# A new order of steps in a transformer encoder kernel, and one mask seed each moved to VectorE and to TensorE

## The chip, the cores and the metric
The kernel runs on one core of a Trainium2 chip. Five engines work side by side, each through its own list of instructions, and wait for each other by semaphores: TensorE (PE; matrix products into PSUM), VectorE (DVE), ScalarE (ACT; activations, with function tables that have to be loaded), GpSimd (POOL) and SyncE (SP), which here issues transfers. The metric is the time of one execution on the device in microseconds (us), lower is better.

## The reference
The input is 16 sequences of 256 rows of 128 numbers. A first layer norm gives `xn`; the result is `x + encoder(xn) + experts(xn)`. The encoder has four layers; in each:

```python
xn = layer_norm(x, ln1_w[i], ln1_b[i])
x = x + mha(xn, mask, in_proj_w[i], in_proj_b[i], out_proj_w[i], out_proj_b[i])
xn = layer_norm(x, ln2_w[i], ln2_b[i])
h = jax.nn.gelu(xn @ ffn1_w[i].T + ffn1_b[i], approximate=False)
x = x + (h @ ffn2_w[i].T + ffn2_b[i])
```

`mha` is attention with 16 heads of width 8, a causal mask and a linear position bias; a final layer norm closes the encoder. The experts are one attention of 8 heads over the same rows, with projections cut to segments, and no feed-forward.

## The kernel before
One sequence in one layer is a **unit**: the encoder has 64 of them (4 layers x 16 sequences), the experts 16. The kernel is a software pipeline written by hand: slot `s` of a plan holds, one after another, steps of the units s-2 to s+3, and every engine walks through the same list (`slot_steps`) and issues of each step its own part. So the list sets the order on each engine, and an engine that waits for a step holds up all that stands behind it in its list. Two slots make a round; the rounds stand in loops.

The way of a unit: `ln`, `rstd`, `xn` (norm, on VectorE and POOL), `xt` and `xt+` (transpose on TensorE; scale and bias on ScalarE), `qk` and `y` (queries and keys; their bias on ScalarE), `hi` and `lo` (split into two parts for precision), `hi>` (both parts to DRAM), `smax>`/`smaxp` and `stack>` (transfers that stack them per head, by SyncE and POOL; the first two for the maxima, the last for the scores), 12 steps `max` (score products with the mask as a second product `identb` x `maskb`, line 1022, and a reduction on VectorE, line 768), `negt`, `negt+`, `row>` (the row of negated maxima, as a row of the queries), 12 steps `exp` (a 128x512 score product, line 1052, and the exponential on ScalarE, line 918), four steps `pv` (probabilities by values, line 1075, in column strips of 32), `pv+` (copy, line 818), `ot`, `ot+` (division by the sums), `at`, `at+`, `op`, `op+` (projection and residual), `rstd2`, `xn2`, `xt2`, `xt2+`, `f1` and `gelu` in two halves of two blocks, `f2` in two halves, `f2+`. In the last layer `end` and `end+` work the final norm and `store` writes it.

**Seeds.** Of the 12 score tiles of a unit, 8 cross the diagonal (numbers 0, 2, 3, 5, 6, 8, 9, 11). For these ScalarE first writes the mask `masktf` into the PSUM bank (line 943) and the score product adds to it. There are two such banks (`exp_ps`), used in turn, so the seed of tile k+2 follows the exponential of tile k, and waits for its end. `SEEDER` names the engine for each tile.

**Banks.** Seven more PSUM banks: 0 and 1 (`dense`), 2 to 4 (`mxp`), used by the maxima in turn (2 + k % 3), and one for `pv`. `Plan.banks` gives each other step its bank; `take` makes TensorE wait until the last reader of a bank is done. Before, `xt`, `qk`, `negt`, `f2` use bank 1, `v`, `at`, `op`, `xt2` bank 0, `ot` bank 4, `f1` banks 0 and 1.

Of the kernel before, what the change touches and what calls it, by code (L numbers as in the profile page):

```python
# [22 lines left out]
BF16 = mybir.dt.bfloat16  # L23
# [4 lines left out]
P = 128  # L28
# [23 lines left out]
class Plan:  # L52
# [21 lines left out]
    def slot_steps(self, s, last_layer):  # L74
# [3 lines left out]
        def at(names, unit):  # L78
            return [(name, unit) for name in names.split()]
# [4 lines left out]
        if self.causal:  # L84
            end, end2, store = (at(k, s - 2) if last_layer else [] for k in ("end", "end+", "store"))
            return (
                part("exp", s, 0, 1) + at("ot", s - 1) + at("ln rstd", s + 2) + at("ot+", s - 1) + at("v v+", s + 1)
                + at("w:v xn", s + 2) + part("f2", s - 2, 0, 1) + at("w:w2", s - 1) + at("f2+", s - 2)
                + end + at("at at+", s - 1)
                + part("exp", s, 2) + at("w=w1", s - 1) + part("max", s + 1, 0, 1) + at("xt", s + 2)  # L90
                + part("exp", s, 3) + part("max", s + 1, 2, 3) + at("xt+", s + 2) + at("op xb", s - 1)
                + at("stack>", s + 1)
                + part("exp", s, 4) + at("w=v", s + 2) + part("max", s + 1, 4) + at("op+ rstd2 w=w2 xb2", s - 1)
                + at("w:o", s) + at("qk", s + 2)
                + part("exp", s, 5) + part("max", s + 1, 5, 6) + at("y", s + 2) + at("w:qk", s + 3)
                + at("hi lo hi>", s + 2)
                + part("exp", s, 6) + part("max", s + 1, 7, 8) + end2 + at("xn2", s - 1)
                + part("exp", s, 7) + part("max", s + 1, 9, 10)
                + part("exp", s, 8) + part("max", s + 1, 11)
                + part("exp", s, 9) + at("w=o", s) + at("xt2 xt2+", s - 1) + part("pv", s, 0, 1)  # L100
                + part("exp", s, 10) + at("w=qk", s + 3) + at("negt negt+ row>", s + 1) + at("smaxp smax>", s + 2)
                + part("exp", s, 11) + part("f1", s - 1, 0, 1) + part("gelu", s - 1, 0, 1) + at("w:w1", s)
                + part("pv", s, 2, 3) + at("pv+", s) + store)
# [25 lines left out]
    "xt": 1, "qk": 1, "v": 0, "at": 0, "op": 0, "xt2": 0, "negt": 1, "f2": 1, "ot": 4, "f1": (0, 1)})  # L129
# [1099 lines left out]
```

## Time and profile before

| | |
|---|---|
| median of 3 runs | 1633.32 us (1630.77 to 1640.77) |
| profiled execution | 1632.11 us |
| its span | 1630.3 us |
| granted TensorE clock, mean over the span | 0.968 of full speed |
| TensorE / ScalarE / VectorE busy | 1420.4 / 1225.0 / 1124.3 us |

A timeline row gives start, duration, engine, line, operation, tiles written and read, shapes and count, and in brackets how long the engine was idle before it and what ended this. Rows of one kind in a row are merged. Matmuls are pipelined: the duration of one is from its start to its modelled end, and the distance of two ends is what it adds. The chain of work that ended last is followed back from the last instruction to what released each step; its pieces are such distances.

### The profile page before, as it was taken

To read this page: it belongs to the slowest core of one execution; us is meant where nothing else is said; L and a number is where in the kernel's file an instruction comes from. 1 tells how busy PE (TensorE), PEld (TensorE's weight loads), DVE (VectorE), ACT (ScalarE), POOL (GpSimd) and SP (SyncE) were. 2 spreads that over 40 slices of the span, in tenths; PEclk is the share of its full clock that TensorE was granted. 3 is DMA by queue.
4 is the path that set the end of the run, shared out by engine and by line. 5 is a ranking of instruction groups with operands and counts; after the bars stand their busy time and mean duration, and the time that the engine had idled before them with its cause. 6 is when DMAs were issued, how large, how long until landed. Compare 5 with 4: busy or idle time off the path is not lost.

```text
span 1630.3 us, 39578 instructions
## 1 busy us (share of the span) xinstructions
PE 1420.4 (87%) x10656; PEld 949.4 (58%) x10720; DVE 1124.3 (69%) x2850; ACT 1225.0 (75%) x2165; POOL 613.5 (38%) x1052
## 2 busy tenths in 40 slices
PE   0677787679999999999999999999999999999994
PEld 0445554346666666666666666666666666666653
DVE  6566666457777777777777767777677777777762
ACT  3233333248889889999898888888989888888883
POOL 5232323223334333333333333333333345555533
PEclk9899889789999999999999999999999999999997
DMA  4333333144444444544444445444444444444430
GB/s 131 101 103 93 104 90 114 43 128 125 119 118 117 125 131 120 141 129 118 119 130 121 123 117 135 125 127 117 120 128 128 128 129 123 122 123 123 125 85 11
DMA packets 106535, 187.80 MB, mean 115 GB/s; under 512 B 20104, under 2 KB 72456, under 8 KB 106448
## 3 DMA queue, kind: packets, MB, share of 16 engines
q1 hardware_dynamic: 91632, 150.45, 33.3%
q0 software_dynamic: 14848, 36.72, 8.4%
q8 instruction: 21, 0.34, 0.1%
q14 instruction: 34, 0.28, 0.1%
HBM read 120.87 MB, written 65.01 MB: 114 GB/s over the span
## 4 chain that ended last, share of the span: by engine, by line
PE 52%; DVE 18%; issue 14%; DMA 8%; POOL 1%; ACT 1%; SPq 1%; DVEq 1%; POOLq 0%; ACTq 0%
PE pvp L1075 12%; PE exp_ps L1052 7%; DVE negm L768 7%; PE mxp L1018 6%; PE dense L1116 5%; PE dense L1104 5%; DMA blocks<-split_L 5%; PE dense L964 5%; PE mxp L1022 2%; DVE xn L736 2%; PE dense L1093 2%; DVE ost L818 2%; PE mxp L964 2%; PE dense L1003 2%; PE dense L993 2%
## 5 line engine op out<-in xcount | busy, mean ns | idle before, releaser
L918 ACT ACTIVATE probs<-exp_ps 128x512 f32<-128x512 f32 x896 | 525.7, 593 | 283.6 <-PE exp_ps L1052 279.7
L768 DVE TENSOR_REDUCE negm<-mxp 128x2 f32<-128x512 f32 x896 | 568.4, 682 | 74.1 <-remote 38.3
L1052 PE MATMUL exp_ps<-qbd_l,kst_l 128*128 128x512 f32 x768 | 367.8, 495 | 9.6 <-issue 5.0
L1018 PE MATMUL mxp<-blocks,qst 104*128 104x512 f32 x768 | 326.4, 453 | 29.7 <-DVE negm L768 16.5
L943 ACT ACTIVATE exp_ps<-masktf 128x512 f32<-128x512 f32 x513 | 308.8, 602 | 22.6 <-DVE rest L840 6.4
L556 POOL TENSOR_SCALAR veps<-mv 128x2 f32<-128x2 f32 x144 | 31.7, 220 | 540.5 <-DVE mv L727 537.2
L1022 PE MATMUL mxp<-maskb,identb 128*128 128x256 bf16 (+1 forms) x704 | 222.1, 315 | 0.0
L818 DVE COPY ost<-pvp 128x512 f32<-128x512 f32 x80 | 55.3, 691 | 205.6 <-PE pvp L1075 205.6
L1018 PEld LDWEIGHTS mxp<-blocks,qst 104*128 104x128 f32 x768 | 148.5, 193 | 83.0 <-DVE negm L768 43.4
L1075 PE MATMUL pvp<-probs,vst_l 128*32 128x256 f32 (+1 forms) x4096 | 194.2, 330 | 0.6 <-ACT probs L918 0.6
L1052 PEld LDWEIGHTS exp_ps<-qbd_l,kst_l 128*128 128x128 f32 x768 | 144.4, 195 | 41.1 <-issue 32.7
L1022 PEld LDWEIGHTS mxp<-maskb,identb 128*128 128x128 bf16 x768 | 75.1, 98 | 156.9 <-issue 135.1
L1075 PEld LDWEIGHTS pvp<-probs,vst_l 128*32 128x32 f32 x4096 | 115.1, 110 | 77.6 <-ACT probs L918 26.3
L592 POOL TENSOR_TENSOR lo<-y,hi 128x512 fp32r<-128x512 f32 x80 | 102.6, 1283 | 134.8 <-DVE hi L743 134.8
L736 DVE TENSOR_SCALAR xn<-state,mv,rstd 128x128 f32 (+1 forms) x288 | 133.6, 503 | 20.6 <-POOL rstd L558 19.1
L964 PE MATMUL dense<-ident,xn 128*128 128x128 f32 x288 | 62.4, 301 | 77.9 <-DVE xn L736 73.1
L1116 PE MATMUL dense<-wc_l,hid 128*128 128x128 f32 x1024 | 124.9, 274 | 1.0 <-ACT hid L939 1.0
L1104 PE MATMUL dense<-xnt,wc_l 128*128 128x256 f32 x512 | 122.6, 383 | 0.7 <-ACT xnt L932 0.7
L623 POOL DMA_DIRECT2D blocks<-split_L x128 | 68.8, 544 | 144.0 <-DVE negt L807 113.2
L1116 PEld LDWEIGHTS dense<-wc_l,hid 128*128 128x128 f32 x1024 | 119.5, 192 | 1.7 <-ACT hid L939 1.6
L558 POOL TENSOR_TENSOR rstd<-veps,half 128x2 f32<-128x2 f32 x144 | 102.7, 713 | 12.0
L1104 PEld LDWEIGHTS dense<-xnt,wc_l 128*128 128x128 f32 x512 | 98.3, 192 | 14.2 <-ACT xnt L932 1.1
(94 smaller groups left out, 2014.0 us busy)
## 6 DMA issues: line engine op xcount, KB each, us to landing
split_L<-hi SPq DMA_DIRECT2D x256, 128.0 KB, 2.1
qst<-split_L SPq DMA_DIRECT2D x64, 384.0 KB
kst_l<-split_L SPq DMA_DIRECT2D x64, 384.0 KB
qbd_l<-split_L SPq DMA_DIRECT2D x256, 96.0 KB
split_L<-lo POOLq DMA_DIRECT2D x128, 128.0 KB, 2.1
blocks<-split_L POOLq DMA_DIRECT2D x128, 96.0 KB, 4.3
blocks<-split_L SPq DMA_DIRECT2D x128, 96.0 KB
split_F<-hi SPq DMA_DIRECT2D x64, 128.0 KB, 2.1
```

The source lines that it names most:

```text
L558: pool.tensor_tensor(rstd[:, k, s, :], veps[:, k, s, :], half[:, 0:NT], ALU.pow).then_inc(done, 1)
L736: last = dve.tensor_scalar(xn[:, k, s, t, :], source[:, t, :], mv[:, k, s, t, 0:1], rstd[:, k, s, t:t + 1], ALU.subtract, ALU.mult)
L768: dve.tensor_reduce(heads[:, g, first:first + count], bank[MAX_BANK + k % 3].rearrange("p (h t) -> p h t", h=count), AX.X, ALU.max, negate ...
L918: act.activation(probs[:, g, ch, :], exp_ps[:, k % 2, :], ACT.Exp, scale=plan.scale).then_inc(q.b_exp, 1)
L943: act.activation(exp_ps[:, bank, :], masktf.rearrange("p h t -> p (h t)"), ACT.Copy)\
L964: last = pe.transpose(out_bank[0:src.shape[1], k * width:(k + 1) * width], src, ident[:, :])
L1018: pe.matmul(o, qst[0:BIAS_END, g, qt * P:(qt + 1) * P], kbd[0:BIAS_END, first:first + count, g, 0:keys], start=True, stop=True, skip_group ...
L1022: last = pe.matmul(diagonal, identb[:, :], maskb[:, 0:count, :], start=False, stop=True, skip_group_check=True)
L1052: last = pe.matmul(o, kst[plan.name][:, s, g, kt * P:(kt + 1) * P], rhs, start=seeder not in ("ACT", "DVE"), stop=True, skip_group_check=True)
L1075: last = pe.matmul(pvp[32 * col:32 * col + 32, region * T + q0:(region + 1) * T], v, src, start=lead, stop=fin_, skip_group_check=True, ti ...
L1104: last = pe.matmul(o[:, (f % 2) * T:(f % 2 + 1) * T], wc["L"][:, C_W1 + f * P:C_W1 + (f + 1) * P], xnt[:, 1, s, :], start=True, stop=True)
L1116: last = pe.matmul(o[:, k * D:(k + 1) * D], hid[:, s, f, k * P:(k + 1) * P], wc["L"][:, C_W2 + f * D:C_W2 + (f + 1) * D], start=(f == 0), ...
```

## The change
The list of a slot is written anew for the encoder (the experts' stays), the banks of its steps are other ones, seed 0 goes to VectorE (the list has a `seed` step for it, for unit s+1, in front of `pv 3`), tile 2 is no longer seeded: after its score product TensorE adds `identb` x `masktb`, a bfloat16 copy of the mask that POOL makes once. POOL's share of the final norm (`end_rstd`, `end_sum`) becomes steps of their own at the end of a slot.

```diff
         if self.causal:
...
             return (
-                part("exp", s, 0, 1) + at("ot", s - 1) + at("ln rstd", s + 2) + at("ot+", s - 1) + at("v v+", s + 1)
-                + at("w:v xn", s + 2) + part("f2", s - 2, 0, 1) + at("w:w2", s - 1) + at("f2+", s - 2)
-                + end + at("at at+", s - 1)
...
+                at("w:v", s + 2) + at("w:w1", s - 1) + at("w:qk", s + 3) + at("w:o", s) + part("f1", s - 2, 1)
+                + at("hi>", s + 2) + at("w=o", s) + at("w=w1", s - 1) + at("v", s + 1) + at("xn", s + 2)
+                + at("at+ ot", s - 1) + at("xt", s + 2) + at("ot+", s - 1) + at("v+", s + 1) + part("f2", s - 2, 0)
+                + at("at", s - 1) + at("xt+", s + 2) + at("ln", s + 3)
+                + part("exp", s, 0, 1) + at("stack>", s + 1) + at("w:w2", s - 1) + at("w=v", s + 2) + at("w=qk", s + 3)
+                + at("op+ op", s - 1) + at("qk", s + 2) + part("max", s + 1, 0) + at("y", s + 2) + part("max", s + 1, 1)
...
+                + part("exp", s, 11) + at("lo", s + 2) + part("gelu", s - 1, 0) + at("negt+ negt", s + 1)
+                + part("gelu", s - 1, 1) + part("pv", s, 2) + part("seed", s + 1, 0) + part("pv", s, 3) + at("pv+", s)
+                + at("row>", s + 1) + store + at("xb", s) + at("rstd", s + 3) + end_rstd + end_sum)
...
-    "xt": 1, "qk": 1, "v": 0, "at": 0, "op": 0, "xt2": 0, "negt": 1, "f2": 1, "ot": 4, "f1": (0, 1)})
+    "xt": 0, "qk": 4, "v": 4, "at": 2, "op": 2, "xt2": 0, "negt": 3, "f2": 1, "ot": 3, "f1": (0, 1)})
...
-SEEDER = {0: "ACT", 2: "ACT", 3: "ACT", 5: "ACT", 6: "ACT", 8: "ACT", 9: "ACT", 11: "ACT"}
+SEEDER = {0: "DVE", 2: "PE", 3: "ACT", 5: "ACT", 6: "ACT", 8: "ACT", 9: "ACT", 11: "ACT"}
...
+                        if seeder == "PE":
+                            last = pe.matmul(o, identb[:, :], masktb.rearrange("p h t -> p (h t)"), start=False, stop=True,
+                                             skip_group_check=True)
```

On ScalarE, from the GELU of one unit into the next, in the last rounds (written out, without a loop); before:

```order
L939 ACTIVATE hid<-dense,wc_l 128x256 x4
L918 ACT_TABLE_LOAD
L918 ACTIVATE probs<-exp_ps 128x512
L943 ACTIVATE exp_ps<-masktf 128x512
L918 ACTIVATE probs<-exp_ps 128x512
L943 ACTIVATE exp_ps<-masktf 128x512
L925 ACTIVATE attnt<-dense 128x256
L918 ACTIVATE probs<-exp_ps 128x512 x2
```

and now (line numbers are those of the changed kernel, 4 higher):

```order
L943 ACTIVATE hid<-dense,wc_l 128x256 x4
L929 ACTIVATE attnt<-mxp 128x256
L908 ACTIVATE xnt<-dense,wa_l 128x256
L922 ACT_TABLE_LOAD
L922 ACTIVATE probs<-exp_ps 128x512 x2
L947 ACTIVATE exp_ps<-masktf 128x512
L915 ACTIVATE y<-mxp,wa_l 128x256 x2
L922 ACTIVATE probs<-exp_ps 128x512 x2
```

The attention copy and the normalised input now stand ahead of the table load and the first exponential; exponential 0 has no seed behind it.

On TensorE, the same place; `dense<-xnt,wc_l` is `f1`, `dense<-wc_l,hid` is `f2`; before:

```order
L964 MATMUL dense<-ident,negm 16x128 x2
L1052 MATMUL exp_ps<-qbd_l,kst_l 128x512
L1104 MATMUL dense<-xnt,wc_l 128x256 x4
L1075 MATMUL pvp<-probs,vst_l 32x256 x4
L1075 MATMUL pvp<-probs,vst_l 32x128 x4
L1075 MATMUL pvp<-probs,vst_l 32x256 x4
L1075 MATMUL pvp<-probs,vst_l 32x128 x4
L1052 MATMUL exp_ps<-qbd_l,kst_l 128x512 x2
L964 MATMUL mxp<-ident,ost 128x128 x4
L1003 MATMUL dense<-wa_l,xnt 128x128 x2
L1116 MATMUL dense<-wc_l,hid 128x128 x8
L964 MATMUL dense<-ident,attn 128x128 x2
```

and now:

```order
L968 MATMUL mxp<-ident,negm 16x128 x2
L1082 MATMUL pvp<-probs,vst_l 32x256 x4
L1082 MATMUL pvp<-probs,vst_l 32x128 x4
L1082 MATMUL pvp<-probs,vst_l 32x256 x4
L1082 MATMUL pvp<-probs,vst_l 32x128 x4
L1111 MATMUL dense<-xnt,wc_l 128x256 x2
L1007 MATMUL mxp<-wa_l,xnt 128x128 x2
L968 MATMUL mxp<-ident,ost 128x128 x4
L968 MATMUL dense<-ident,xn 128x128 x2
L1123 MATMUL dense<-wc_l,hid 128x128 x4
L968 MATMUL mxp<-ident,attn 128x128 x2
L1056 MATMUL exp_ps<-qbd_l,kst_l 128x512 x2
```

One half of `f1` moved behind the last `pv`, the score products 0 and 1 moved behind `ot`, `xt`, the first half of `f2` and `at`.

On TensorE a few steps on; before, `qk` (`dense<-xnt,wa_l`) stands between maxima 4 and score 5:

```order
L1022 MATMUL mxp<-maskb,identb 128x2x128
L993 MATMUL dense<-xnt,wa_l 128x256 x2
L1052 MATMUL exp_ps<-qbd_l,kst_l 128x512
L1018 MATMUL mxp<-blocks,qst 128x512
L1022 MATMUL mxp<-maskb,identb 128x2x128
L1018 MATMUL mxp<-blocks,qst 128x512
L1022 MATMUL mxp<-maskb,identb 128x512
L1052 MATMUL exp_ps<-qbd_l,kst_l 128x512
```

and now `op` and `qk` stand ahead of maxima 0, and score 2 has a mask product:

```order
L1100 MATMUL mxp<-wc_l,attnt 128x128 x2
L997 MATMUL mxp<-xnt,wa_l 128x256 x2
L1022 MATMUL mxp<-blocks,qst 128x512
L1026 MATMUL mxp<-maskb,identb 128x512
L1022 MATMUL mxp<-blocks,qst 128x512
L1026 MATMUL mxp<-maskb,identb 128x2x128
L1056 MATMUL exp_ps<-qbd_l,kst_l 128x512
L1059 MATMUL exp_ps<-masktb,identb 128x512
L1056 MATMUL exp_ps<-qbd_l,kst_l 128x512
L1022 MATMUL mxp<-blocks,qst 128x512
L1026 MATMUL mxp<-maskb,identb 128x2x128
L1022 MATMUL mxp<-blocks,qst 128x512
```

`qk` writes bank 4, which maxima 2 (the third `mxp<-blocks,qst` row) use next.

## Rows read from the trace of the kernel before

**Rows 1.** The page: busy times; and the chain that ended last, by engine.
```profile
PE 1420.4 (87%) x10656; PEld 949.4 (58%) x10720; DVE 1124.3 (69%) x2850; ACT 1225.0 (75%) x2165; POOL 613.5 (38%) x1052
...
PE 52%; DVE 18%; issue 14%; DMA 8%; POOL 1%; ACT 1%; SPq 1%; DVEq 1%; POOLq 0%; ACTq 0%
```

**Rows 2.** Timeline, VectorE, line 818: start us, us, engine, line, operation, count, [idle before, releaser].
```profile
359.17 0.69 DVE L818 COPY ost<-pvp 128x512 f32<-128x512 f32 x1 [2.09 <-PE pvp L1075]
...
1339.54 0.69 DVE L818 COPY ost<-pvp 128x512 f32<-128x512 f32 x1 [2.92 <-PE pvp L1075]
...
1602.68 0.69 DVE L818 COPY ost<-pvp 128x512 f32<-128x512 f32 x1 [7.66 <-PE pvp L1075]
```

**Rows 3.** Timeline, ScalarE, from one unit's end into the next.
```profile
708.25 0.60 ACT L918 ACTIVATE probs<-exp_ps 128x512 f32<-128x512 f32 x1 [0.85 <-PE exp_ps L1052]
...
710.02 1.28 ACT L939 ACT_TABLE_LOAD   x1
711.32 1.56 ACT L939 ACTIVATE hid<-dense,wc_l 128x256 f32<-128x256 f32 x4
...
714.19 0.60 ACT L918 ACTIVATE probs<-exp_ps 128x512 f32<-128x512 f32 x1
714.82 0.60 ACT L943 ACTIVATE exp_ps<-masktf 128x512 f32<-128x512 f32 x1
715.36 0.58 ACT L918 ACTIVATE probs<-exp_ps 128x512 f32<-128x512 f32 x1
...
716.51 0.37 ACT L925 ACTIVATE attnt<-dense 128x256 f32<-128x256 f32 x1
...
716.77 1.26 ACT L918 ACTIVATE probs<-exp_ps 128x512 f32<-128x512 f32 x2
...
718.60 0.55 ACT L904 ACTIVATE xnt<-dense,wa_l 128x256 f32<-128x256 f32 x1
...
721.16 0.83 ACT L911 ACTIVATE y<-dense,wa_l 128x256 f32<-128x256 f32 x2
```

**Rows 4.** Chain in order of time, 700 to 740 us: start us, us, what.
```profile
707.79 0.43 PE exp_ps L1052
...
708.67 1.73 PE dense L1104 x8
710.40 1.48 PE pvp L1075 x32
...
713.82 1.79 PE dense L1116 x16
715.61 0.22 PE dense L964 x2
715.83 0.23 PE exp_ps L1052
...
717.63 0.12 PE mxp L1022
717.76 0.23 PE mxp L1018
717.99 0.23 PE mxp L1022
718.22 0.44 PE dense L1093 x4
```

**Rows 5.** Timeline, TensorE: a product that waited for ScalarE.
```profile
719.29 1.10 PE L993 MATMUL dense<-xnt,wa_l 128*128 128x256 f32 x4
```

**Rows 6.** The page, costliest groups: shapes, count | busy, mean ns | idle before.
```profile
L768 DVE TENSOR_REDUCE negm<-mxp 128x2 f32<-128x512 f32 x896 | 568.4, 682 | 74.1 <-remote 38.3
```

**Rows 7.** Chain in order of time, 789 to 812 us: a transfer.
```profile
788.61 5.20 DMA blocks<-split_L
```

**Rows 8.** Timeline, VectorE, in the tail.
```profile
1610.49 0.42 DVE L830 TENSOR_TENSOR state<-dense,xb 128x256 f32<-128x256 f32 x1 [2.93 <-POOL xb L635]
```

More of the change, by code:

```diff
@@ L84, in slot_steps @@
         if self.causal:
-            end, end2, store = (at(k, s - 2) if last_layer else [] for k in ("end", "end+", "store"))
+            end, end_rstd, end2, end_sum, store = (
+                at(k, s - 2) if last_layer else [] for k in ("end", "end_rstd", "end+", "end_sum", "store"))
             return (
-                part("exp", s, 0, 1) + at("ot", s - 1) + at("ln rstd", s + 2) + at("ot+", s - 1) + at("v v+", s + 1)
-                + at("w:v xn", s + 2) + part("f2", s - 2, 0, 1) + at("w:w2", s - 1) + at("f2+", s - 2)
-                + end + at("at at+", s - 1)
[L90 to L103, printed above, removed]
@@ new lines, in slot_steps @@
+                + at("op+ op", s - 1) + at("qk", s + 2) + part("max", s + 1, 0) + at("y", s + 2) + part("max", s + 1, 1)
+                + part("exp", s, 2, 3) + part("max", s + 1, 2) + at("hi", s + 2) + part("max", s + 1, 3)
+                + part("exp", s, 4) + part("max", s + 1, 4) + part("pv", s, 0) + part("max", s + 1, 5, 6)
+                + part("exp", s, 5, 6) + part("f2", s - 2, 1) + at("xn2", s - 1) + at("f2+", s - 2)
+                + end + at("smaxp", s + 1)
+                + part("exp", s, 7) + part("max", s + 1, 7, 8) + at("xb2", s - 1) + part("max", s + 1, 9)
@@ new lines, in slot_steps @@
+                + part("exp", s, 8) + at("xt2+", s - 1) + part("pv", s, 1) + at("smax>", s + 2) + at("w=w2 xt2", s - 1)
+                + part("max", s + 1, 10)
+                + part("exp", s, 9) + at("rstd2", s - 1) + part("max", s + 1, 11) + end2
+                + part("exp", s, 10) + part("f1", s - 1, 0)
+                + part("exp", s, 11) + at("lo", s + 2) + part("gelu", s - 1, 0) + at("negt+ negt", s + 1)
+                + part("gelu", s - 1, 1) + part("pv", s, 2) + part("seed", s + 1, 0) + part("pv", s, 3) + at("pv+", s)
@@ L316, in build @@
         masktf = sb("masktf", [P, 4, P])
+        masktb = sb("masktb", [P, 4, P], BF16)
         split = {p.name: nc.dram_tensor(f"split_{p.name}", [2, 2, p.hg, COPIES, p.dh, GROUPS * T], F32,
@@ L566, in steps @@
                         inverse_deviation(q, "C", u, s)
-                    elif step == "end":
+                    elif step == "end_rstd":
                         b = u - (LAYERS - 1) * BATCH
@@ L577, in steps @@
                         pool.tensor_tensor(rest[:, b, :, :], rest[:, b, :, :], bias, ALU.add).then_inc(s_end_rest, 1)
-                    elif step == "end+":
+                    elif step == "end_sum":
                         b = u - (LAYERS - 1) * BATCH
@@ L1137, in encoder @@
                 next_round(n)
-            pe.wait_ge(s_init, 12)
+            pe.wait_ge(s_init, 13)
             pe.wait_ge(s_initv, 1)
```

1 line of the change is left out of this document (added).

## The prediction

> **What bounds the kernel now.** The busy times first [rows 1]: TensorE 87% of the span, ScalarE 75%, VectorE 69%. Nothing is full, so the chain of work that ended last decides: TensorE holds 52% of it, VectorE 18%, "issue" 14%, DMA 8%, ScalarE 1%. The encoder repeats one pattern, once for each of its 64 units. The copy of a unit's attention output (line 818) marks one period [rows 2]: from 359.17 to 1339.54 us there are 50 periods, mean 19.61 us; then 13 to 1602.68, mean 20.24 us, in which the final norm is worked too. Before them lie 359 us (experts and filling), behind them 27.6 us. The span is 1630.3 us and the profiled execution 1632.1 us; the median of the runs shown is 1633.32, so 1.2 us above it.
>
> Inside a period TensorE's own work, taken from end to end of its products [rows 4]: 12 score products at 0.23, 12 maxima products at 0.23 with 4 masks at 0.23 and 8 at 0.12, values and output projection 0.44 each, queries and keys 0.87 (half of the 1.73 for the first feed-forward, which has twice the products), feed-forward 1.73 and 1.79, four probability-value steps at 0.74, six pairs of transposes at 0.22. That is about 17.0 us. The other 2.3 to 2.6 us are waits and refills. One wait shows the price of a refill [rows 3, 5]: the activation begun at 718.60 ends at 719.15, the product that waited ends at 719.29+1.10 = 720.39, 1.24 us later, for 0.87 of streaming: 0.37 extra. And the score product behind a probability-value step ends 0.43 after it, where 0.23 is normal [rows 4]: 0.20 for leaving that step.
>
> **The change, part by part.** (1) Two of eight seeds leave ScalarE. A seed followed by another activation takes 714.82 to 715.36 = 0.54 us, and it delays the exponential ahead of it to 0.63 [rows 3]; so 2 x 0.6 = 1.2 us less per unit on an engine that holds 1% of the chain [rows 1]. Alone this gains nothing. (2) One seed goes to VectorE, after the copy of negated maxima: not in the trace; at least nothing, since the engine idles 31% of the span; at most about 0.69 us, the 128x512 copy with one side in PSUM [rows 2], its nearest row, which I take. It runs while TensorE does the last probability-value step, whose copy stands behind it and can't begin before T+1.1 (T is where a unit's last exponential ends). Hidden. (3) One seed becomes a mask product: 0.23 us as the same 128x512 mask [rows 4].
>
> (4) The order. I walk one period with the durations of [rows 3, 4]; times are from T.
> ScalarE: table load and four GELU activations end at 2.88 in before (710.02 less 0.02 is T there). Now TensorE did score product 11 (ends T-0.62: 0.03 [rows 3, 4] and the exponential of 0.58), transposes 0.22 and pv 2, 0.74, so at 0.34 it starts pv 3: 1.08, leaving it 1.28, second half of feed-forward 1 (0.87): 2.15. The second GELU pair starts at 2.2 and not 2.10: end 2.95. Values, two pairs of transposes and one more take TensorE to 3.25.
> The first half of feed-forward 2 needs the GELU: 2.95+0.37+0.90 = 4.2. Behind it in TensorE's queue stands the transpose of attention: 4.42. And ScalarE has, ahead of its first exponential, what waits for this: the attention copy (starts 4.46; the next activation 0.26 later), the normalised input (0.55, ends 5.27), the table load (1.28) [rows 3]. Exponential 0 starts at 6.58. In before it started at 4.19 (714.19 against 710.00). These 2.4 us of delay are the change's largest cost.
> Then exponential 1 at 7.12, seed 3 at 7.75 (ends 8.35), the pair of query and key activations 8.29 to 9.12 [rows 3]. TensorE meanwhile ends queries and keys at 5.27+1.24 = 6.51, maxima 0 and 1 at 7.33, score 2 with its new mask at 8.0, and waits for seed 3: score 3 ends 8.35+0.37+0.23 = 8.95. Maxima 2 now uses the bank of queries and keys (bank 4), so it waits for both activations: 9.12+0.37+0.23 = 9.72.
> From there TensorE streams: its mask 0.12, eight scores 1.84, six maxima with short mask 2.22, three with long 1.38, pv 0 and pv 1 1.48, leaving each 0.40, half of feed-forward 2 0.90, transposes 0.22, half of feed-forward 1 0.87: 9.43 in all, end 19.15. ScalarE is ready there (six seeds keep it below this). Plus 0.62 to the end of exponential 11: **T+19.77**.
>
> So the gains (normalised input ready early, pv 2 ahead of the last exponential, the projection's waits gone from VectorE's queue) about equal the losses: a mask 0.23, two places more on the stream where a pv step is left, 0.40, and the two waits before maxima 2. VectorE's twelve reductions at 0.68 [rows 6] are followed by the copy of high parts, norm and residual; the latest reduction that TensorE needs (maxima 8 for 11) ends over 1 us ahead in my walk. With 0.4 us less slack it would show.
>
> (5) Transfers. In before a DMA row of 5.20 us [rows 7] ends where maxima 0 start, one reason why the mean is 19.61. Now SyncE issues the stack for maxima ahead of the row of maxima, hence about 1.6 us before T, and maxima 0 start at 6.5, not 5.9: this wait should go. SyncE's queue stacks queries and keys behind the high parts (about T+13 to 15.5): 8 us ahead of their use. If that cover were gone, the row of maxima would be late next, then score 0.
> (6) Tail: an addition waited 2.93 us for POOL's xb, which stood behind the final norm [rows 8]; xb is now made a slot earlier: -3 us. Experts unchanged.
>
> Sum against the profiled execution: 50 x (19.77 - 19.61) = +8; 13 periods with the final norm: POOL and VectorE carry the same work, +1; tail -3. 1632.1 + 6 = **1638 us**.
>
> A rule speaks of the price of leaving a step. What rows show: pv steps take 1.48 for two with no visible price on entering, 0.20 on leaving [rows 4]. The Trainium skill, TensorEngine Tiling (Array Packing), Key Properties, says that a change of tiling mode drains TensorE; that would count on entering as well. By this reading two more entries on the stream cost some 0.2 each; the trace agrees for leaving alone.
>
> **The rivals.** (a) Leaving costs nothing here: the 0.20 is seen only where a score product follows; now maxima, transposes and feed-forward follow. Then the stream is 0.40 shorter and the GELU 0.07 earlier: T+19.30, (19.30-19.61) x 50 = -15, 13 x -0.3 = -4, tail -3: **1610**. For it: no row of another follower; against: it is an idle of the array, not a wait of the score. (b) ScalarE was the bound and the two seeds pay in full: 64 x 1.2 = -77: **1555**. Against: 1% of the chain. (c) Entering costs 0.20 too at pv 0 and pv 1: 63 x 0.4 = +25: **1663**, slower. It decides from 0.15 per entry on. Against: 1.48 for two steps. (d) The high parts, the stack of queries and keys and the low parts now move together; if the low parts land later than about T+20.5, SyncE's stack for maxima and the row behind it hold up score 0, by 1 us per us: +1 gives **1701**. For it: the 5.20 us row; against: 3 us of slack. (e) In the last 13 periods POOL's blocks stand behind the final sum, which now comes after all maxima: up to 1 us each, **1651**. (f) The order doesn't matter, as both are bound by the same work: **1633**.
>
> **How the numbers follow.** Forecast 0.40, (a) 0.20, (b) 0.06, (c) 0.11, (d) 0.09, (e) 0.06, (f) 0.08. The forecast's own range is 1622 to 1652 (0.25 us per period either way, the refills of a walk). The range of 8 in 10 reaches past (a) and (c), each with the forecast's own error of a few us: 1598 to 1670; it leaves out (b) and (d). About 1% is what a measurement of this kernel can tell from no change. Faster by over 1% (under 1617): (a), (b), some of the forecast's edge, 0.27. Slower (over 1649.7): (c), (d), half of (e), edge: 0.27. Within: 0.46.
>
> **What would show it.** Period of line 818's successor near 19.8, with little spread; exponential 0 starting 6.4 to 6.8 us after the last exponential's end, ScalarE idle 1.5 us behind the GELU; score 3 and maxima 2 each with an idle, ended by ScalarE; no maxima product waiting for DMA; the product behind each pv step 0.20 late; the seed on VectorE 0.6 to 0.7. Wrong if the first exponential starts before 6, or if TensorE waits after maxima 2: then VectorE or a transfer is the bound.

## The result

The changed kernel takes 1648.74 us, median of 4 runs (1646.89 to 1654.01); the kernel before took 1632.05 us beside it (1629.61 to 1640.77, 4 runs). The ratio is 1.0098, with a 95% interval of 1.0053 to 1.0143: about 1% slower, 10.7 us above the 1638 that the prediction names. Its profiled execution took 1647.52 us, with a span of 1645.0.

The page of the changed kernel, busy times and the chain by engine, answers to [rows 1]:
```profile
PE 1446.2 (88%) x10719; PEld 956.2 (58%) x10784; DVE 1143.3 (69%) x2914; ACT 1146.8 (70%) x2036; POOL 610.3 (37%) x1053
...
PE 63%; ACT 11%; issue 8%; DMA 8%; DVE 4%; SPq 1%; POOL 1%; ACTq 1%; another core or an unknown queue 0%; DVEq 0%; POOLq 0%
```
TensorE works 26 us more, and ScalarE 78 us less, but the two have changed their place in the chain: VectorE's share went from 18% to 4%, and ScalarE, which has less to do than before, now holds 11% of it instead of 1%.

The copies that mark the periods (now line 822), first, 51st and last, in VectorE's timeline of the changed kernel, answer to [rows 2]:
```profile
363.77 0.69 DVE L822 COPY ost<-pvp 128x512 f32<-128x512 f32 x1 [0.45 <-PE pvp L1082]
...
1364.66 0.69 DVE L822 COPY ost<-pvp 128x512 f32<-128x512 f32 x1 [0.36 <-PE pvp L1082]
...
1621.39 0.69 DVE L822 COPY ost<-pvp 128x512 f32<-128x512 f32 x1 [2.31 <-PE pvp L1082]
```
From these starts the span divides as follows (before by [rows 2]):

| stretch | before, us | after, us | difference |
|---|---|---|---|
| up to the first copy | 359.17 | 363.77 | +4.6 |
| 50 periods | 980.37 (19.61 each) | 1000.89 (20.02 each) | +20.5 |
| last 13 periods | 263.14 (20.24 each) | 256.73 (19.75 each) | -6.4 |
| behind the last copy | 27.6 | 23.6 | -4.0 |
| span | 1630.3 | 1645.0 | +14.7 |

The undisturbed periods of the changed kernel alternate between 19.85 and 19.98 us; seven of the first 50 are longer (20.19 to 22.49). Of the last 13, the two at the end are short in both kernels (19.56 and 18.88 before, 19.45 and 17.88 after), since the pipeline runs empty there.

ScalarE's timeline of the changed kernel, from the end of a unit's last exponential (T = 741.36) into the next unit, answers to [rows 3]:
```profile
742.68 1.65 ACT L943 ACTIVATE hid<-dense,wc_l 128x256 f32<-128x256 f32 x4
745.95 0.39 ACT L929 ACTIVATE attnt<-mxp 128x256 f32<-128x256 f32 x1 [1.63 <-PE mxp L968]
746.25 0.56 ACT L908 ACTIVATE xnt<-dense,wa_l 128x256 f32<-128x256 f32 x1
746.83 1.28 ACT L922 ACT_TABLE_LOAD   x1
748.12 1.09 ACT L922 ACTIVATE probs<-exp_ps 128x512 f32<-128x512 f32 x2
749.24 0.60 ACT L947 ACTIVATE exp_ps<-masktf 128x512 f32<-128x512 f32 x1
749.78 0.82 ACT L915 ACTIVATE y<-mxp,wa_l 128x256 f32<-128x256 f32 x2
```
The engine idles 1.63 us behind the GELU, until TensorE has multiplied with its result and transposed. Then it works without a gap, and what it does last there, `y` at 749.78, is what TensorE waits for. The chain in order of time, the same period, answers to [rows 4]:
```profile
742.38 1.06 PE dense L1111 x4
...
744.54 1.06 PE dense L1123 x8
...
750.65 0.50 PE mxp L1022
...
752.34 0.79 PE pvp L1082 x16
753.12 0.43 PE mxp L1022
...
757.13 0.79 PE pvp L1082 x16
757.92 0.37 PE dense L968 x2
...
759.48 0.86 PE dense L1111 x4
760.35 0.36 PE exp_ps L1056
```
From 750.65 on no other engine stands in the chain up to the last score (760.71): this is the stream. What TensorE waited for between 600 and 1200 us, in total, times, longest:
```profile
PE exp_ps L1056 <- DMA qbd_l<-negt: 18.6, 17, 2.4
PE exp_ps L1056 <- ACT exp_ps L947: 6.1, 18, 0.4
PE mxp L1022 <- ACT y L915: 5.4, 21, 0.3
```
The first of the three is new: the first score of a unit waits for the row of negated maxima. In most periods it costs nothing, since maximum 2 waits for `y` behind it anyway: in the period shown score 0 waited 0.59 us for the row, and the period is an undisturbed one. No maximum waits for a transfer in this stretch any more (in [rows 7] one did).

### The profile page after: what moved, and what is told of

It is laid out like the page before. It is cut to its first block, busy times and chain, and to the rows that moved or that the text cites. A ratio compares the mean times of both kernels' runs of the same rounds, so it can differ in the third digit from the quotient of the medians.

```text
span 1645.0 us, 39871 instructions
## 1 busy us (share of the span) xinstructions
PE 1446.2 (88%) x10719; PEld 956.2 (58%) x10784; DVE 1143.3 (69%) x2914; ACT 1146.8 (70%) x2036; POOL 610.3 (37%) x1053
## 4 chain that ended last, share of the span: by engine, by line
PE 63%; ACT 11%; issue 8%; DMA 8%; DVE 4%; SPq 1%; POOL 1%; ACTq 1%; another core or an unknown queue 0%; DVEq 0%; POOLq 0%
PE pvp L1082 12%; PE exp_ps L1056 10%; PE mxp L1022 10%; PE dense L1123 6%; PE dense L1111 6%; PE mxp L1026 6%; ACT probs L922 4%; ACT L922 3%; PE dense L968 3%; DMA qbd_l<-negt 3%; PE mxp L968 3%; ACT y L915 2%; DMA blocks<-negt 2%; DVE negm L772 2%; PE mxp L1007 1%
## 5 line engine op out<-in xcount | busy, mean ns | idle before, releaser
L922 ACT ACTIVATE probs<-exp_ps 128x512 f32<-128x512 f32 x896 | 504.5, 592 | 236.8 <-PE exp_ps L1056 226.6
L1056 PE MATMUL exp_ps<-qbd_l,kst_l 128*128 128x512 f32 x768 | 358.0, 496 | 54.3 <-DMA qbd_l<-negt 26.4
L947 ACT ACTIVATE exp_ps<-masktf 128x512 f32<-128x512 f32 x384 | 231.1, 602 | 12.2
L1082 PE MATMUL pvp<-probs,vst_l 128*32 128x256 f32 (+1 forms) x4096 | 207.0, 331 | 0.0
L654 POOL TENSOR_TENSOR xb<-state,wc_l 128x128 f32<-128x128 f32 x128 | 55.9, 454 | 309.4 <-DVE state L834 309.4
L1123 PE MATMUL dense<-wc_l,hid 128*128 128x128 f32 x1024 | 140.1, 279 | 2.9 <-ACT hid L943 2.2
L1111 PE MATMUL dense<-xnt,wc_l 128*128 128x256 f32 x512 | 139.1, 395 | 1.0 <-ACT xnt L936 1.0
L1123 PEld LDWEIGHTS dense<-wc_l,hid 128*128 128x128 f32 x1024 | 128.8, 191 | 17.8 <-ACT hid L943 4.9
L740 DVE TENSOR_SCALAR xn<-state,mv,rstd 128x128 f32 (+1 forms) x288 | 101.6, 400 | 20.5 <-POOL rstd L562 18.3
L943 ACT ACTIVATE hid<-dense,wc_l 128x256 f32<-128x256 f32 x256 | 105.4, 471 | 3.4 <-PE dense L1111 2.6
```

Source lines behind the costliest of these rows:

```text
L922: act.activation(probs[:, g, ch, :], exp_ps[:, k % 2, :], ACT.Exp, scale=plan.scale).then_inc(q.b_exp, 1)
L943: act.activation(hid[:, s, f, :], bank[plan.banks["f1"][k]][:, (f % 2) * T:(f % 2 + 1) * T], ACT.Gelu, bias=wc["L"][:, C_B1 + f:C_B1 + f + ...
L947: act.activation(exp_ps[:, bank, :], masktf.rearrange("p h t -> p (h t)"), ACT.Copy)\
L1056: last = pe.matmul(o, kst[plan.name][:, s, g, kt * P:(kt + 1) * P], rhs, start=seeder not in ("ACT", "DVE"), stop=True, skip_group_check=True)
L1082: last = pe.matmul(pvp[32 * col:32 * col + 32, region * T + q0:(region + 1) * T], v, src, start=lead, stop=fin_, skip_group_check=True, ti ...
L1111: last = pe.matmul(o[:, (f % 2) * T:(f % 2 + 1) * T], wc["L"][:, C_W1 + f * P:C_W1 + (f + 1) * P], xnt[:, 1, s, :], start=True, stop=True)
```

## The experiments

Every kernel stands against the kernel before, run beside it on the same chip. That one's median was 1632.47 us beside the first four kernels below "after", 1633.29 beside the last three, and 1636.26 beside the four between them; so compare the ratios before the times. Names of steps are those of the slot list. "Order" is the new list with its banks. The periods are worked out from the copies into `ost`, as above.

| kernel | time, us | ratio to before, 95% interval | mean of 50 | mean of last 13 |
|---|---|---|---|---|
| before | 1632.05 | 1 | 19.61 | 20.24 |
| after | 1648.74 | 1.0098 (1.0053 to 1.0143) | 20.02 | 19.75 |
| new order, old seeds | 1732.18 | 1.0608 (1.0588 to 1.0627) | 21.35 | 21.38 |
| old order, new seeds | 1635.66 | 1.0019 (1.0003 to 1.0036) | 19.65 | 20.30 |
| after, q/k in bank 0 | 1627.49 | 0.9955 (0.9936 to 0.9974) | 19.74 | 19.55 |
| after, pv 0 beside pv 1 | 1661.59 | 1.0164 (1.0144 to 1.0184) | 20.27 | 19.99 |
| after, at+ and xt+ behind exp 1 | 1776.02 | 1.0904 (1.0829 to 1.0978) | 21.90 | 22.00 |
| after, w2 load behind the row | 1642.72 | 1.0053 (1.0029 to 1.0076) | 20.02 | 19.83 |
| before, final norm late | 1631.33 | 0.9975 (0.9954 to 0.9997) | 19.57 | 19.82 |
| q/k in bank 0, tile 3 masked by TensorE | 1606.99 | 0.9830 (0.9790 to 0.9871) | 19.47 | 19.05 |
| after, row first | 1638.76 | 1.0043 (1.0022 to 1.0063) | 19.96 | 19.73 |
| bank 0, tile 3, w2 load late | 1604.66 | 0.9815 (0.9786 to 0.9844) | 19.38 | 19.20 |
| bank 0, tile 3, row first | 1622.94 | 0.9935 (0.9908 to 0.9961) | 19.68 | 19.57 |

### The two halves of the change, each alone

In the diffs of this section, "..." at an end marks steps of a line that are left out. New order, old seeds: in the changed kernel
```diff
-SEEDER = {0: "DVE", 2: "PE", 3: "ACT", ...}
+SEEDER = {0: "ACT", 2: "ACT", 3: "ACT", ...}
-    ... + part("pv", s, 2) + part("seed", s + 1, 0) + part("pv", s, 3) + ...
+    ... + part("pv", s, 2) + part("pv", s, 3) + ...
```


> The new order and banks, but all eight seeds with the scalar engine as before. Theory (the walk of the prediction): in the new order ScalarE holds the head of a period, so seed 2 (0.54 us behind exponential 0, and 0.09 more for the exponential's end) delays seed 3 and the pair of query and key activations, which maxima 2 wait for; seed 0 behind exponential 10 delays exponential 11 a little. A period grows from 19.91 by 0.6 to 0.8 us: 40 to 50 us more, about 1693 us, slower than both kernels. Rival (the seeds are nothing, since TensorE bounds the stream): a mask product of 0.23 us less on TensorE, which waits at score 3 anyway: 1640 to 1650 us.

Old order, new seeds: the list and the banks of before, with `SEEDER` of after and
```diff
-                + part("pv", s, 2, 3) + at("pv+", s) + store)
+                + part("seed", s + 1, 0) + part("pv", s, 2, 3) + at("pv+", s) + store)
```


> The order and the banks of before, with the new seeds (0 by VectorE ahead of pv 2, tile 2 as a mask product, six by ScalarE). Theory: TensorE and VectorE's queue bound that order, ScalarE had slack, so the seeds alone give nothing and the product costs at most 0.23 us per unit: 1632 to 1645 us. Rival (two seeds less on ScalarE pay 1.2 us per unit): 1555 us; half of that would be 1595.

In the old order the new seeds are worth nothing: 1635.66 us, 0.2% above before. With the new order they are worth 83 us (1732.18 against 1648.74), 1.3 us a period. So the two do not add up: order alone +100 us, seeds alone +3, both +17. Why the seeds weigh so much in the new order is seen in the kernel with the new order and the old seeds. TensorE's waits for seeds between 600 and 1200 us (6.1 us in 18 waits in the changed kernel), and the chain in order of time at a unit's end:
```profile
PE exp_ps L1056 <- ACT exp_ps L947: 25.3, 48, 0.7
...
740.83 0.61 ACT probs L922
...
741.46 0.04 ACT exp_ps L947
...
741.99 0.59 ACT probs L922
...
742.60 0.04 ACT exp_ps L947
...
743.14 0.59 ACT probs L922
...
743.77 0.86 PE pvp L1082 x16
```
These are exponential 9, the seed of score 11, exponential 10, seed 0 of the next unit and exponential 11. Score 11 waits for its seed, and pv 2 for the exponential behind seed 0; in the changed kernel the last score ends with only exponential 11 left to do. A likely reason is the late start: exponential 0 begins 6.7 us behind T (the end of a unit's last exponential), and eight seeds instead of six have to fit into what is left of the period. Counted from T, `y` ends 0.6 us later than in the changed kernel, and from score 11's end to the next T it is 1.1 us instead of 0.6: undisturbed periods of 20.9 to 21.1 us. The rest of the mean of 21.35 is TensorE's clock. Of the first 50 periods 13 took 22.1 to 22.6 us, and exactly these 13 hold a stretch of 3.4 us in which the granted clock was 0.50 of full speed (1.2 instead of 2.4 GHz); all others had 1.00. One is at 840.0 to 843.4 us, 1.0 us behind the last of three waits of TensorE, for two seeds and `y`, of 0.41, 0.65 and 0.26 us. Such a fall costs some 1.5 us. My figure for this run (1693) was too low by 39 us: I had priced the seeds where they delay `y`, at the head of the unit, had put down "a little" for its tail, and had nothing for the clock.

### The wait in front of maximum 2

```diff
-    "xt": 0, "qk": 4, "v": 4, ...
+    "xt": 0, "qk": 0, "v": 4, ...
```


> The changed kernel with queries and keys in bank 0 instead of 4, so that maxima 2 no longer wait for ScalarE's two activations (y). Theory: maxima 2 follow score 3 at once; a period is 0.4 to 0.6 us shorter: 25 to 35 us less, about 1618 us. Rival (the wait hides another one that comes out right behind, seeds 5 and 6 or VectorE's reductions): under 0.15 us per period, 1640 us or more.

Maximum 2 shares a PSUM bank with the product of queries and keys in the changed kernel and so waits for `y`. With the product in bank 0 the undisturbed periods fall from 19.85 and 19.98 to 19.51 and 19.64 us, and the time by 21 us, to 1627.49: this wait alone makes the difference between 1% slower than before and slightly faster than before (0.9936 to 0.9974). I had expected 1618. What is left at this place, chain in order of time:
```profile
737.91 1.09 ACT probs L922 x2
...
739.02 0.61 ACT exp_ps L947
...
739.68 0.50 PE exp_ps L1056
```
Now score 3 waits for its seed, as the prediction's walk has it (step "waits for seed 3").

```diff
-SEEDER = {0: "DVE", 2: "PE", 3: "ACT", ...}
+SEEDER = {0: "DVE", 2: "PE", 3: "PE", ...}
```
(on top of the edit before)

> The kernel after with q/k's product in bank 0 (the run before this one, 1627.5 us) and tile 3 masked by TensorE, like tile 2, instead of seeded by ScalarE: one mask product of 0.23 us more on TensorE and one seed of 0.6 us less on ScalarE, ahead of score 3. Theory: in the run with bank 0 score 3 waits for ScalarE's seed 3 in most units, by 0.3 to 0.6 us; without the seed it goes behind maximum 1, the wait turns to less than the product's 0.23 us, and a period loses 0.1 to 0.4 us: 1603 to 1621 us. Rival: the stream takes in the 0.23 us in full, since exponential 2 or the maxima's row is late next: 1635 to 1642 us.

1606.99 us: 20.5 us less than with bank 0 alone, and 1.7% below the kernel before. The undisturbed periods are 18.90 to 19.06 us. The chain in order of time:
```profile
749.36 1.44 PE pvp L1082 x32
750.80 1.06 PE dense L1111 x4
...
754.79 0.68 PE mxp L1100 x4
755.47 0.88 PE dense L997 x4
...
757.57 0.23 PE exp_ps L1059
...
758.05 0.23 PE exp_ps L1059
```
Between 739.93 and 761.94 us its pieces belong to TensorE, but for 0.05 us: a second mask product at 0.23 has taken the place of a wait, and the period is now TensorE's own work. In this list that is 18.9 us and not the 17.0 that the prediction took from before: the two mask products are 0.46 of the difference, leaving a pv step in three places 0.5, and most of the rest lies in the first product behind a change of work, which takes longer than the same one further on (0.68 above for the projection, 0.44 in [rows 4]; 0.36 for score 11 behind the half feed-forward, 0.23 elsewhere).

### Where pv 0 stands

```diff
-    ... + part("max", s + 1, 4) + part("pv", s, 0) + part("max", s + 1, 5, 6)
+    ... + part("max", s + 1, 4) + part("max", s + 1, 5, 6)
-    ... + at("xt2+", s - 1) + part("pv", s, 1) + ...
+    ... + at("xt2+", s - 1) + part("pv", s, 0, 1) + ...
```


> The changed kernel with pv 0 moved beside pv 1, so that TensorE leaves the column strips one time less per unit. Theory: 0.20 us for leaving and 0.05 for entering, all on the stream that ends the period: 63 x 0.25 = 16 us less, about 1633 us. Rival (the stream isn't what ends a period, ScalarE's eleven seeds and exponentials are): no change, 1649 us.

I held pv 0 to be a plain loss, one more place where a pv step is left. Moved away, it made the period 0.25 us longer (20.10 and 20.22) instead of shorter. The chain in order of time, and a wait of ScalarE between 600 and 1200 us:
```profile
734.93 0.61 DVE negm L772
...
735.58 0.51 PE mxp L1022
736.09 0.23 PE mxp L1026
...
ACT xnt L936 <- PE dense L968: 37.5, 29, 1.3
```
Maximum 6 (its mask is the long one, 0.23) now waits for VectorE's reduction of maximum 3 to free their bank, 8.8 us in 29 waits, which pv 0 had covered. This accounts for the whole loss. The move takes 0.99 us away in front of maximum 6 (0.79 and 0.20 for leaving), but the wait of 0.30 us stands there, and the product behind it takes 0.51 instead of 0.23: maximum 6 ends only 0.42 us earlier behind T (12.13 for 12.55). Further on the pair takes 1.44 instead of 0.79, 0.65 more. ScalarE's longer wait with `xt2+` (19.5 us in 30 waits in the changed kernel) has no part in it: from 735.58 us to the last score no other engine stands in the chain. My theory for this run was right on the price of leaving and overlooked the bank.

### Where at+ and xt+ stand

```diff
-                + at("at+ ot", s - 1) + at("xt", s + 2) + ...
-                + at("at", s - 1) + at("xt+", s + 2) + at("ln", s + 3)
-                + part("exp", s, 0, 1) + at("stack>", s + 1) + ...
+                + at("ot", s - 1) + at("xt", s + 2) + ...
+                + at("at", s - 1) + at("ln", s + 3)
+                + part("exp", s, 0, 1) + at("at+", s - 1) + at("xt+", s + 2) + at("stack>", s + 1) + ...
```


> The kernel after, but on ScalarE the copies at+ and xt+ (with the table load between them and the first exponential) stand behind exponential 1 of the next unit again, as before, and not ahead of exponential 0. The prediction called the 2.4 us by which they delay exponential 0 the change's largest cost. If that cost is real, the kernel gains: up to 1.5 us a unit would take it to about 1570 us, and even 0.3 us a unit to 1630. The rival: the delay is only a name for where the copies lie. TensorE fills the same time with products of its own, and with the copies behind exponential 1 op, q/k and value products and so y come later by the two exponentials and a seed, about 1.5 us, of which the stream behind y takes 0.3 to 0.5 us a unit on: 1665 to 1680 us.

Exponential 0 starts 4.8 us behind T instead of 6.8, and the kernel takes 1776.02 us, by the ratios 8% more than after, some 130 us. Three things are at work. The undisturbed period is 20.6 us, some 0.7 above that of after. TensorE's longest wait (between 600 and 1200 us) and what it waits for, in ScalarE's timeline and in the chain:
```profile
PE mxp L1100 <- ACT attnt L929: 52.9, 27, 2.0
...
807.24 0.37 ACT L929 ACTIVATE attnt<-mxp 128x256 f32<-128x256 f32 x1
...
807.75 0.68 PE mxp L1100 x4
```
The copy `at+` stands behind two exponentials and a seed, and the projection, q/k's product and the maxima stand behind it: maximum 2 ends 10.4 us behind T (811.20 - 800.81), where in after it ends 9.8. The wait is at the projection, not at `y` as I wrote. Over 63 periods this is some 44 us. Second, TensorE's granted clock fell to 0.50 of full speed 25 times in these 63 periods, for 3.4 or 6.8 us each and 106 us in all, mostly within 1.5 us behind the start of the product that had waited 2.0 us for `at+`; in after it did so twice, in before once. By an estimate from these figures this costs up to 53 us, half of the 106. Third, the row of maxima is late in some periods (next section). Second and third together make the periods of 22 to 27 us. No run separates the three.

### The long periods

Seven of the first 50 periods of after are longer than 20.1 us, by 7.3 us together; in all seven the first score starts 0.1 to 0.4 us behind the landing of the row. In one of them the chain in order of time is
```profile
696.92 6.56 DMA wc_l<-in_wc_l
...
703.76 3.40 DMA qbd_l<-negt
```
SyncE stood in the step that loads the weights w2 until a load of 6.56 us was over, and the row of maxima was behind it in its list.
```diff
-    ... + at("smax>", s + 2) + at("w=w2 xt2", s - 1)
+    ... + at("smax>", s + 2) + at("xt2", s - 1)
-                + at("row>", s + 1) + store + ...
+                + at("row>", s + 1) + at("w=w2", s - 1) + store + ...
```


> The kernel after, but SyncE's step that loads the next layer's w2 weights stands behind the step that writes the maxima's row to the stacked keys (row), not ahead of it. In the trace of after SyncE stood at that weight load at some layer crossings, row went out late, and these periods took 20.3 to 22.5 us where the undisturbed ones take 19.85 to 19.98. Theory: the late rows are that queue place; the long periods of the first 50 shrink to the undisturbed ones, some 7 us in all: 1641 us. Rival: the long periods come from the weights' own transfers, or from the row's landing behind the stacks' bytes: no difference, 1647 to 1650 us.

This is not settled by the times: 1642.72 us fits the theory's 1641, but the mean of the first 50 periods is 20.02, as in after, and the intervals of the two ratios overlap. The waits for the row fell (26.4 to 20.2 us in the whole span), and some long periods went, yet one of 22.04 us came up, with another cause for the late row (and a fall of the granted clock to 0.50 behind it). First GpSimd's timeline, then the chain in order of time, of this kernel:
```profile
954.82 1.22 POOL L609 DMA_DIRECT2D split_L<-lo  x2 [3.56 <-issue]
...
955.47 3.74 DMA split_L<-lo
...
960.79 4.20 DMA qbd_l<-negt
```
The low parts go out 3.6 us late; `smax>` waits until they have landed, and the row stands behind `smax>`. That is the mechanism of the prediction's rival (d), at single places. So the row was put ahead of both:
```diff
-    ... + part("pv", s, 1) + at("smax>", s + 2) + at("w=w2 xt2", s - 1)
+    ... + part("pv", s, 1) + at("w=w2 xt2", s - 1)
-                + at("row>", s + 1) + store + ...
+                + at("row>", s + 1) + at("smax>", s + 2) + store + ...
```


> The kernel after, but on SyncE the step that writes the maxima's row (row) stands ahead of the one that writes the next-but-one unit's blocks for the maxima (smax) and ahead of the w2 load. Smax waits for the parts of keys and queries to be written to DRAM, and in the run with the copies behind exponential 1 some rows went out only behind it. Theory: in the long periods of after the row is late by its place in the queue or by the bytes ahead of it; with nothing ahead of it they shrink to the undisturbed 19.85 to 19.98, 7 us in all, and maximum 0 still finds its blocks landed, since they have some 5 us to spare and leave 2 to 3 us later: 1641 us. Rival: the blocks leave too late and maximum 0 waits for them as in the kernel before, 1 us or more in most units: 1700 us and above.

In this edit only `smax>` moved; the w2 load stayed ahead of the row (the expectation says otherwise, which is an error of mine). 1638.76 us, and the 50 periods 19.96: the longest is 21.03, and all but three of them are within 0.2 us of the undisturbed ones from the second on. What TensorE waited for, 600 to 1200 us:
```profile
PE mxp L1022 <- DMA blocks<-split_L: 23.2, 28, 1.6
...
PE exp_ps L1056 <- DMA qbd_l<-negt: 0.8, 2, 0.5
```
The row's wait is gone, from 18.6 to 0.8 us, so it was its place behind `smax>` that cost most. That place has two costs. The row, 16 KB, took 2.2 us from issue to landing in before and in this run, and 4.0 us in after, where the stacks for the maxima go out ahead of it (medians of some 47 transfers each, 400 to 1340 us). And it can go out late: in four of the seven long periods of after it was issued 1.9 to 3.4 us behind T, where 0.2 to 0.3 is usual, and landed 3.4 to 4.4 us on; in the other three it was issued in time and took 5.3 to 5.7 us. Behind the w2 load's move four of the five long periods that follow the first one are of the second kind.

One more cost hides in the longest period, 22.49 us: the granted clock fell to 0.50 from 1347.8 to 1351.2 us, at the end of the first score's wait of 2.20 us for the row. In the other 49 it was 1.00 throughout. A period whose row landed just as late, without a fall, took 21.24, so this fall costs some 1.3 us of the 7.3.

A wait of the maxima for their blocks, 0.8 us a unit, has come instead. In the undisturbed periods it costs nothing, since TensorE would wait for `y` right behind it anyway; the three longer periods are those in which it is longest (1.6 to 1.9 us). In time the gain is small: behind the first period the other 49 took 978.4 us instead of 982.9, and the intervals of the two ratios overlap. Where that cover is gone, the wait costs. The last two kernels take this up with q/k in bank 0 and tile 3 masked by TensorE:
```diff
-    ... + at("smax>", s + 2) + at("w=w2 xt2", s - 1)
+    ... + at("smax>", s + 2) + at("xt2", s - 1)
-                + at("row>", s + 1) + store + ...
+                + at("row>", s + 1) + at("w=w2", s - 1) + store + ...
```


> The kernel of the last run (q/k in bank 0, tile 3 masked by TensorE: 1607 us) with SyncE's w2 load behind the row. Theory: its undisturbed periods (18.9 to 19.1) stay and part of the long ones at the layer crossings (20.8, 23.5, 22.2, 23.1, 23.2) shrinks: 5 to 15 us, 1592 to 1602 us. Rival: their lateness is in the landing, not in the queue: 1607 us.

And from this kernel to the last:
```diff
-    ... + at("smax>", s + 2) + at("xt2", s - 1)
+    ... + at("xt2", s - 1)
-                + at("row>", s + 1) + at("w=w2", s - 1) + store + ...
+                + at("row>", s + 1) + at("smax>", s + 2) + at("w=w2", s - 1) + store + ...
```


> The same kernel (q/k in bank 0, tile 3 masked by TensorE) with the row ahead of both the blocks' step and the w2 load on SyncE. Theory, if the row's lateness comes from the queue: all long periods shrink, 14 to 16 us: 1591 to 1595 us. Rival: with a period of 19 us the blocks leave too late for maximum 0: 1615 us and above.

With the w2 load late: 1604.66 us, not to be told from 1606.99 without it (the intervals of the ratios, 0.9786 to 0.9844 and 0.9790 to 0.9871, nearly coincide), so that place in SyncE's list is worth nothing that was measured. In both kernels every one of the first 50 periods above 22 us (22.2 to 23.5) holds a fall of the granted clock to 0.50; there are four such periods without the load's move and two with it. The kernel with the load late has the lowest median of all here, 1.85% below before. With the row first: 1622.94 us, 18 us slower. Its undisturbed 18.9 us are hardly met any more; most periods are 19.2 to 20.3, and the maxima wait for their blocks (20.9 us in 27 waits). What was free in the changed kernel is paid for here.

### The last 13 periods

In the kernel before:
```diff
-                + part("exp", s, 6) + part("max", s + 1, 7, 8) + end2 + at("xn2", s - 1)
+                + part("exp", s, 6) + part("max", s + 1, 7, 8) + at("xn2", s - 1)
...
-                + part("exp", s, 8) + part("max", s + 1, 11)
+                + part("exp", s, 8) + part("max", s + 1, 11) + end2
...
-                + part("pv", s, 2, 3) + at("pv+", s) + store)
+                + part("pv", s, 2, 3) + at("pv+", s) + store
+                + (at("end_sum", s - 2) if last_layer else []))
```


> The kernel before, order, seeds and banks, but of the final norm VectorE's normalization stands behind maximum 11 instead of behind maxima 7 and 8, and GpSimd's two last operations of it stand at the end of the slot, behind the steps that issue and fill the next unit's blocks. It touches the last 13 units alone. Theory: in these units before took 20.24 us a period where its others took 19.61 because VectorE and GpSimd had the final norm ahead of maxima 9 and 10 and ahead of the blocks; after has both behind them and took 19.75. So the last 13 periods come down to 19.7 to 19.9 us, and the time by 5 to 7 us: about 1627 us. Rival: the last 13 periods of after are shorter for another reason (its stores, its seeds): no difference, 1632 us.

Of GpSimd's part only the last sum was moved; its inverse deviation stayed where it was. The 13 periods fall from 20.24 to 19.82 us, 5.4 us in all, the 50 others stay (19.57), and the ratio is 0.9975 (0.9954 to 0.9997). The chain of the kernel before in order of time had the final norm's normalization ahead of `xn2`, for which TensorE's transposes waited:
```profile
1413.39 0.18 DVE tmp L858
...
1414.16 0.34 DVE tmp L858
```
With the gap between them that is 1.1 us. In the run it has left the chain, and between 1340 and 1600 us TensorE's waits for normalised input (`xn`, `xn2`) fell from 9.0 to 2.9 us, which is about the gain. The periods, but for the last two, are still 0.3 us or more above the others; in after there is no such difference. With the old order and the new seeds the same 13 periods took 20.30 us, so the seeds have no part in it.

## Why the prediction came out as it did

The time lies inside the range, and 10.7 us above the forecast, which sat between errors of both signs. Step by step:

- **The two seeds alone gain nothing: right.** 1635.66 us in the old order; rival (b) has fallen there. But the reason given, an engine with 1% of the chain, holds only for the old order. In the new one the same two seeds are worth 83 us, of which a part is the clock. (b) priced them at 77 us against the wrong comparison; that the two figures are close is chance.
- **The prices of the two new operations: right.** VectorE's seed was bounded by 0.69 us; VectorE's timeline:
```profile
741.42 0.67 DVE L818 COPY exp_ps<-masktf 128x512 f32<-128x512 f32 x1
```
  It is hidden, as said. The mask product takes 0.23 us in the chain.
- **The walk of a period: right in its places, short in its sum.** From T: `at+` at 4.59 (predicted 4.46), exponential 0 at 6.76 (6.58), seed 3 ends at 8.48 (8.35; 749.24 + 0.60), `y` ends at 9.24 (9.12), maximum 2 ends at 9.79 (9.72), score 11 at 19.35 (19.15). The idle behind the GELU (1.5 predicted, 1.63) and both waits of TensorE for ScalarE are there (18 and 21 of them in the 30 periods between 600 and 1200 us). The undisturbed period is 19.91 in the mean instead of 19.77. In the stream of the period shown, 9.56 us from the end of maximum 2 where 9.43 was put, the terms that were too small are the two single pv steps, 0.79 each instead of 0.74, and score 11 behind the half feed-forward, 0.36 instead of 0.23; the transposes behind pv 1 gave 0.05 back. Two figures of the working don't follow from their terms: six maxima with short masks at 0.23 and 0.12 are 2.10 and not 2.22 (each took 0.36, so 2.16), and score 2 with its mask would end at 7.33 + 0.46 = 7.79 and not 8.0; nothing hangs on the second.
- **Leaving a pv step costs 0.20 whatever follows: right, and rival (a) has fallen.** Maximum 5 behind pv 0 takes 0.43 (0.23 is normal), the transposes behind pv 1 take 0.37 (0.22), and the half feed-forward behind pv 3 takes 1.06 (0.87). Rival (c), the same price on entering, has fallen as to size: a single step is 0.79, and the pairs are 1.44, so a unit's four steps take 3.02 us against 2.96 before, 0.06 more for the further entry and not 0.40. The Trainium skill, TensorEngine Tiling (Array Packing), Key Properties, says that switching the mode drains TensorE; the trace agrees for the way out of the strips, with 0.15 to 0.20 us, and shows under 0.1 us on the way in.
- **"These 2.4 us of delay are the change's largest cost": wrong.** Undoing the delay costs some 130 us, 44 of them in the undisturbed periods. It isn't a cost but the price of having the projection and q/k's product early. The largest cost that could be taken away was the next one in the walk, the bank of queries and keys, 21 us, and then seed 3, 20.5 us; the walk has both waits, but the prediction's text doesn't price them one by one.
- **"VectorE's reductions end over 1 us ahead": wrong at one place.** When pv 0 and its 0.99 us were taken away in front of maxima 5 and 6, maximum 6 waited 0.3 us, so the slack there is about 0.7 us.
- **Transfers: half right.** The wait of maximum 0 for its blocks is gone, as said. What was missed is what the same move did to the row: it now stands behind `smax>` and the w2 load on SyncE, goes out late whenever one of these waits, and takes 4.0 us to land instead of 2.2. Seven long periods hold 7.3 us of this, some 1.3 of it by a fall of the clock; with `smax>` behind the row the waits for it fell from 18.6 to 0.8 us. The text had this as rival (d), for low parts that land late, with 3 us of slack and every unit in mind; it comes at single units.
- **The last 13 periods: wrong sign.** +1 us was put, -6.4 measured. The reason given, that both engines carry the same work, leaves out where it stands: the normalization ahead of `xn2` was on the path in before. Moving it in the kernel before gained 5.4 us. Rival (e), blocks that are late, came in one of the 13 periods, where maximum 0 waited 1.08 us.
- **The tail: right.** -3 predicted, -4.0 measured. An answer to [rows 8], which had 2.93 us of waiting for GpSimd's `xb`:
```profile
1626.08 0.42 DVE L834 TENSOR_TENSOR state<-mxp,xb 128x256 f32<-128x256 f32 x1 [2.40 <-PE mxp L1100]
```
  It now waits for the product instead, and begins 4.69 us behind the last copy, where it was 7.81: 3.1 of the 4.0 us.
- **The start: +4.6 us, not in the prediction, and open.** The first copy stands anywhere from 355.8 to 364.9 us in the kernels run here, most of which share the list of after, so a single trace can't tell such a difference from scatter.

The sum: the walk's error, 50 x 0.14 = +7.0; the late rows, +7.3; the first period, which is 1.9 shorter than an undisturbed one; the last 13 periods, -7.4 against what was put; the tail, -1.0; the start, +4.6. That is +8.6 us, and the span is longer than predicted by 1645.0 - 1636.3 = 8.7. So that the forecast lies within 1% of the time is in part luck: the last 13 periods, forecast with the wrong sign, took 7.4 us off what the walk and the rows had put on. The prediction has no term for TensorE's clock. In before and after that is harmless, with no fall and one fall in the first 50 periods; in the two slowest kernels it is not.

## What to carry to other kernels

Walk the next period from the moment at which the last one ends, and then price every wait in the walk by itself: here two waits of 0.3 us that a bank number and a table entry had made were worth 41 us, more than twice what the changed kernel had lost, and without them it is 1.7% faster than the kernel before. (The old order with tile 3 masked by TensorE did not run, so how much of this the order itself brings is not shown.) A relief of an engine is worth what the order makes of it (3 us lost in one order, 83 us gained in the other), so measure it together with the order. In an in-order queue look at what stands behind a waiting transfer, and what covers a wait today: a pv step in front of a maximum, or a wait for `y` behind a late block, looks like waste and is cover. And when a period grows by more than its waits, look at the granted clock in it before you look for another wait.

## What the runs showed of the hardware

- A product group in column strips costs 0.15 to 0.20 us when it is left, whether a 104x512, a 128x128 or a 128x256 product follows, and less than 0.1 us to enter.
- A product that adds a bfloat16 mask of 128x512 to a bank takes 0.23 us of TensorE; to seed the bank takes 0.60 us on ScalarE and 0.67 us on VectorE. For tile 3, whose seed TensorE waited for, the product in place of ScalarE's seed gained 20.5 us, though TensorE is the busiest engine. A seed of tile 3 on VectorE did not run.
- The row of negated maxima, 16 KB and the smallest transfer of a unit, lands 2.2 us behind its issue in the median when it goes out ahead of the stacks for the maxima, and 4.0 us when it goes out behind them.
- The granted TensorE clock falls to 0.50 for 3.4 or 6.8 us inside a kernel that is otherwise at 1.00, behind waits of TensorE. In the kernel with the new order and the old seeds the 13 periods with a fall took 22.1 to 22.6 us, and the others, but for the first, 20.9 to 21.3.
